# Four output projections of an attention block moved ahead of the scores on TensorE

## The chip, the cores and the metric

The kernel runs on one core of a Trainium2 chip. The metric is the device time of one execution in microseconds (us). A core has the engines PE (TensorE, matrix products), DVE (VectorE), ACT (ScalarE), POOL (GpSimd) and SP (SyncE, which issues the DMAs here). Each works through its own queue of instructions; semaphores order them against each other.

## The reference

Eight sequences of 128 tokens with 512 channels go through a gated cross-attention to a context and then through a gated feed-forward network (FFN) with 4-bit weights. Cut to what matters:

```python
# cross-attention, 32 query heads, 8 key/value heads, d = 128
q = rope(layernorm(x) @ Wq); k = rope(ctx @ Wk); v = ctx @ Wv
logits = 30 * tanh(q @ k.T * 0.0884 / 30)
weights = softmax(where(mask, logits, -1e30))
x = x + tanh(g_xattn) * ((weights @ v) @ Wo)
# FFN, weights (q - zero - 1) * scale, groups of 128 rows
h = layernorm(x)
x = x + tanh(g_ffn) * ((silu(h @ Wg) * (h @ Wu)) @ Wd)
```

## The kernel before, in words

Everything is float32 in accuracy: each operand of a matrix product is split into a rounded part (`_hi`) and the rest (`_lo`), and `split_matmul` (lines 50 to 54) makes one product of three matmuls. ACT makes the `_hi` part, DVE or POOL the `_lo` part.

The attention runs in 64 steps, one for each of 8 key/value heads g and 8 sequences b, step s = 8g + b (`SLOTS` = 64, `TAIL` = 56 is the first step of the last head). They are pipelined over slots, 0 to 66. Every engine has a function `slot(s)` that writes its instructions by hand in a fixed order, and `all_slots` calls it for each slot. On PE (line 1239) slot s does:

1. `transpose_k(s-1)`, one small matmul; the Q projection `make_q(s+4)`, 12 matmuls, if there is one left: `has_q_job(s)` is true up to slot 59; `make_kv(s)`, 12 shorter matmuls for keys and values of step s;
2. the scores of step s-1 into `ps_s`, 3 matmuls. They wait for the semaphore `qk_split`, raised by DVE's `kT_lo` (line 982) at the end of `split_qk`;
3. the P·V product of step s-2, after two matmuls into `ps_tot` for the row sums;
4. from slot 61 on, `norm2_T`, four transposes of the FFN's normalised input; in slots 65 and 66 the first gate and up matmuls of the FFN;
5. the output projection of step s-3 into `ps_o`, 12 matmuls. It waits for `a_split`, raised by POOL's `aT_lo` (line 548), and for `acc_done`.

The other engines in the last eight slots, in the order of their queues:

- ACT (line 704): `scale_share` (step s-4's projection out of `ps_o`), `round_q` and `round_k` of s-1, `round_p` of s-2, `aT_hi` of s-3, `v_hi` of s, `cap_and_exp` of s-1 (tanh and exponential), from slot 61 `norm2_hi`, and in slot 61 `round_ffn` (lines 653 and 654). `scale_share` waits for `o_done` and for the residual sum before.
- POOL (line 535): `add_share` (adds that share to the residual `acc`, line 533), `p_rest` (`p_lo` of s-2, line 526), `aT_lo` of s-3 (line 548), `apply_mask` of s-1 (line 472), `invert_std2` (line 497); in slot 60 also `scale` (line 503) and in slot 62 `rest` (lines 509 and 511), both for the FFN's first weights. `p_rest` waits for ACT's rounding of the masked probabilities of s-2.
- DVE (line 985): `split_qk` of s-1 (`qT_lo` line 980, `kT_lo` line 982), `norm2_apply` (`xn`, line 968), the rope of the keys, `moments2_of`, the reciprocal of the row sums and `attn` of s-2 (line 1028), transpose and row sums of the probabilities of s-1 (lines 1034 and 1037). In slots 59 and 61 it also unpacks FFN weights (lines 925 and 928) at the end.

The lines in which the waits of this text are written:

```python
# POOL, slot(s)
                    if TAIL <= s < SLOTS:
                        p_rest(s)
...
                        pool.wait_ge(a_rounded, s - 2)
                        nc.gpsimd.tensor_tensor(aT_lo[:], attn[:], aT_hi[:].bitcast(F32),
                                                ALU.subtract).then_inc(a_split, 1)
# ACT
                def round_p(s):
                    act.wait_ge(masked, s + 1)
# PE, scores in slot(s)
                        pe.wait_ge(qk_split, s)
```

Of the kernel before, what the change touches and what calls it, by code (L numbers as in the profile page):

```python
# [17 lines left out]
B = 8  # L18
T = 128
# [3 lines left out]
HG = 4  # L23
D = 128
GC = HG * D
SLOTS = KV * B
# [30 lines left out]
def flamingo_block(nc, x, ctx_in, mask, g_xattn, g_ffn, Wq, Wk, Wv, Wo,  # L57
# [16 lines left out]
    with ExitStack() as here:  # L74
# [225 lines left out]
        def runs(s):  # L300

            return 0 <= s < SLOTS
# [6 lines left out]
        with nc.Block() as block:  # L309
# [815 lines left out]
            def _(pe):  # L1125
# [110 lines left out]
                prep(7)  # L1236
                make_q(3)

                def slot(s):
                    if runs(s - 1) and s != SLOTS:  # L1240
                        transpose_k(s - 1)
                    if 0 < s and has_q_job(s):
                        make_q(s + AHEAD)
                    if runs(s):
                        make_kv(s)
                    if s == 0:
                        make_q(AHEAD)
                    if runs(s - 1):

                        pe.wait_ge(qk_split, s)  # L1250
                        wait(pe, tanh_done, s - 1)
                        split_matmul(nc, ps_s[:].rearrange("p (h t) -> p h t", h=HG), kT_hi[:], kT_lo[:],
                                     qT_hi[:], qT_lo[:], True, True).then_inc(s_done, 1)
                    if runs(s - 2):

                        vb = (s - 2) % 4
                        pe.wait_ge(p_split, s - 1)
                        wait(pe, norm_done, s - 2)
                        if s == 2:
                            pe.wait_ge(fold_done, 2)  # L1260
                        pe.wait_ge(p_summed, s - 1)
                        nc.tensor.matmul(ps_tot[:, 0:GC // 32], fold[:], partial[:], start=True, stop=True).then_inc(tot_done, 1)
                        mm = split_matmul(nc, ps_pv[:], v_hi[:, vb, :], v_lo[:, vb, :], p_hi[:], p_lo[:], True, True)
                        mm.then_inc(pv_done, 1)
                    if s == TAIL + 9:

                        pe.wait_ge(gate_centred, 1)
                        pe.wait_ge(w_split, 1)
                        pe.wait_ge(prep2_lo, HALF)
                        pe.wait_ge(q_roped, SLOTS)  # L1270
                        pe.wait_ge(qk_split, SLOTS)
                        gate_up(0, 0, 0, (0, 1))
                    if s == TAIL + 10:

                        gate_up(0, 0, 0, (2, 3))
                    if s >= TAIL + 5:
                        norm2_T(s - TAIL - 5)
                    if s == SLOTS - 1:
                        transpose_k(s)
                    if runs(s - 3):  # L1280

                        wp = ((s - 3) // B) % 2
                        if (s - 3) % B == 0:
                            pe.wait_ge(wo_split, ((s - 3) // B + 1) * HG)
                        pe.wait_ge(a_split, s - 2)
                        wait(pe, acc_done, s - 3)
                        for h in range(HG):
                            mm = split_matmul(nc, ps_o[:], aT_hi[:, h * T:(h + 1) * T],
                                              aT_lo[:, h * T:(h + 1) * T],
                                              wo_hi[wp][:, h, :], wo_lo[wp][:, h, :], h == 0, h == HG - 1)  # L1290
                        mm.then_inc(o_done, 1)
                    if s == TAIL + 10:
                        pe.wait_ge(norm_done, SLOTS)
                        norm2_T(6)
# [83 lines left out]
```

## Time and profile before

| | |
|---|---|
| median of 3 runs | 803.22 us |
| lowest and highest | 801.55 and 806.28 us |
| span of the profiled execution, first to last instruction | 802.9 us |
| mean granted TensorE clock | 0.980 |
| attention slots 60 to 63 in that execution | 561.1 to 605.6 us |

The span lies within the times of the runs, 0.3 us below their median. Times in the trace count from the first instruction. Matmuls are pipelined and a row's duration includes the time in the pipe, so the distance of two starts tells what one costs. The granted clock is a share of 2.4 GHz; 0.50 is the lower level, 1.2 GHz. A number behind an operation in brackets is the idle time of the engine ahead of it, with the instruction that ended it. "fp32r" is the rounded float format of the split parts.

### The profile page before, as it was taken

Reading aid. Unit: us, or ns where it says so; the run is one execution under the profiler, and the core shown is the slowest. Engines: PE = TensorE matmul, PEld = TensorE weight load, DVE = VectorE, ACT = ScalarE, POOL = GpSimd, SP = SyncE. Lnnn points to the kernel's source line nnn. Section 1 sums busy time; section 2 is a strip of 40 time slices with the busy share of each in tenths; the row PEclk is TensorE's granted clock in tenths of the full one; section 3 lists DMA queues with packets and bytes.
Section 4 is the critical chain, followed back from the end, with each engine's and each line's share of the span. In section 5 each row is a group of like instructions: output and inputs, shape, how many; then the busy total and the mean of one; then the engine's idle time right before and its main releaser. Section 6 shows DMA issues by size and latency. Waiting matters only on the chain.

```text
span 802.9 us, 11837 instructions
## 1 busy us (share of the span) xinstructions
PE 748.9 (93%) x3650; PEld 618.8 (77%) x3650; DVE 665.4 (83%) x1226; ACT 424.1 (53%) x823; POOL 478.6 (60%) x367
## 2 busy tenths in 40 slices
PE   3879999999999999999999999989668689999998
PEld 2657888888888888888888888878556468888786
DVE  7589999999999999999999999996887687787531
ACT  3475655665565556556556555545444344554520
POOL 4486666566566557556655755576766456656400
PEclk9999999999999999999999999999889899999999
DMA  8601002000200300020020003010110134442011
GB/s 287 199 0 54 1 27 106 0 27 2 105 2 27 105 0 27 5 102 21 8 104 2 27 29 104 8 41 0 26 38 1 46 87 97 102 105 48 0 66 39
DMA packets 57136, 41.70 MB, mean 52 GB/s; under 512 B 22938, under 2 KB 44442, under 8 KB 57082
## 3 DMA queue, kind: packets, MB, share of 16 engines
q1 hardware_dynamic: 57082, 41.03, 17.2%
q8 instruction: 27, 0.44, 0.2%
q14 instruction: 27, 0.22, 0.1%
HBM read 38.90 MB, written 2.11 MB: 51 GB/s over the span
## 4 chain that ended last, share of the span: by engine, by line
PE 85%; DVE 9%; issue 3%; POOL 2%; ACT 1%; DMA 0%; SPq 0%; DVEq 0%; ACTq 0%; POOLq 0%
PE ps_o L52 8%; PE ps_o L53 8%; PE ps_o L54 8%; PE bank_q L52 7%; PE bank_q L54 7%; PE bank_q L53 7%; PE ps_pv L52 3%; PE ps_s L52 3%; PE bank_kv L54 3%; PE bank_kv L52 3%; PE bank_kv L53 3%; PE ps_s L53 3%; PE ps_s L54 3%; PE bank_q L1147 3%; PE bank_q L1148 3%
## 5 line engine op out<-in xcount | busy, mean ns | idle before, releaser
L480 POOL TENSOR_TENSOR q_sin<-q_sin,q_tab 128x512 f32<-128x512 f32 x64 | 84.5, 1320 | 82.8 <-ACT q_sin L623 82.8
L472 POOL TENSOR_TENSOR probs<-probs,keepT 128x512 f32<-128x512 f32 x64 | 83.8, 1309 | 58.8 <-ACT probs L695 58.6
L548 POOL TENSOR_TENSOR aT_lo<-attn,aT_hi 128x512 fp32r<-128x512 f32 x64 | 85.7, 1338 | 51.8 <-ACT aT_hi L718 51.8
L52 PE MATMUL bank_q<-xT_hi,wq_hi 128*128 128x512 f32 x256 | 107.9, 421 | 3.0 <-DVE xT_lo L828 2.0
L52 PE MATMUL ps_o<-wo_hi,aT_hi 128*128 128x512 f32 x256 | 101.7, 397 | 1.8 <-POOL aT_lo L548 1.1
L980 DVE TENSOR_TENSOR qT_lo<-q_rot,qT_hi 128x512 fp32r<-128x512 f32 x64 | 97.0, 1515 | 6.9 <-ACT qT_hi L674 6.9
L53 PE MATMUL bank_q<-xT_lo,wq_hi 128*128 128x512 f32 x256 | 102.1, 399 | 0.0
L54 PE MATMUL bank_q<-xT_hi,wq_lo 128*128 128x512 f32 x256 | 102.0, 398 | 0.0
L53 PE MATMUL ps_o<-wo_lo,aT_hi 128*128 128x512 f32 x256 | 100.9, 394 | 0.0
L54 PE MATMUL ps_o<-wo_hi,aT_lo 128*128 128x512 f32 x256 | 100.7, 393 | 0.0
L622 ACT COPY q_sin<-bank_q 64x512 f32<-64x512 f32 x64 | 37.4, 584 | 49.3 <-PE bank_q L54 47.2
L52 PEld LDWEIGHTS bank_q<-xT_hi,wq_hi 128*128 128x128 f32 x256 | 49.1, 192 | 17.9 <-DVE xT_lo L828 2.4
L690 ACT ACTIVATE capped<-ps_s 128x512 f32<-128x512 f32 x64 | 38.3, 599 | 43.1 <-PE ps_s L54 43.0
L952 DVE SCALAR_TENSOR_TENSOR later_sum<-bank_q,gate_s,first_sum 128x512 f32<-128x512 f32 (+1 forms) x44 | 32.9, 748 | 33.5 <-PE bank_q L1148 20.1
L52 PEld LDWEIGHTS ps_o<-wo_hi,aT_hi 128*128 128x128 f32 x256 | 48.7, 190 | 13.1 <-POOL aT_lo L548 1.3
L54 PEld LDWEIGHTS bank_q<-xT_hi,wq_lo 128*128 128x128 f32 x256 | 48.7, 190 | 11.8
L54 PEld LDWEIGHTS ps_o<-wo_hi,aT_lo 128*128 128x128 f32 x256 | 48.8, 190 | 10.7
L53 PEld LDWEIGHTS ps_o<-wo_lo,aT_hi 128*128 128x128 f32 x256 | 48.8, 191 | 10.3
L53 PEld LDWEIGHTS bank_q<-xT_lo,wq_hi 128*128 128x128 f32 x256 | 49.1, 192 | 8.8
L520 POOL TENSOR_TENSOR gate_sum<-later_sum 128x512 f32<-128x512 f32 (+1 forms) x22 | 33.2, 1509 | 33.2 <-DVE later_sum L952 33.2
L841 DVE TENSOR_TENSOR bank_q<-bank_q,q_tab 128x512 f32<-128x512 f32 x64 | 44.1, 689 | 7.2 <-ACT q_sin L623 7.2
L1028 DVE TENSOR_TENSOR attn<-ps_pv,r_tot 128x512 f32<-128x512 f32 x64 | 44.3, 692 | 4.9 <-POOL aT_lo L548 2.2
(239 smaller groups left out, 2199.6 us busy)
## 6 DMA issues: line engine op xcount, KB each, us to landing
wo_raw<-in_Wo SPq DMA_DIRECT2D x8, 1024.0 KB, 5.4
wq_raw<-in_Wq SPq DMA_DIRECT2D x7, 1024.0 KB, 5.4
packed<-in_gate_q SPq DMA_DIRECT2D x40, 64.0 KB, 2.2
packed<-in_up_q SPq DMA_DIRECT2D x40, 64.0 KB, 2.2
packed<-in_down_q SPq DMA_DIRECT2D x10, 256.0 KB, 3.2
acc<-in_x SPq DMA_DIRECT2D x8, 256.0 KB, 5.1
wkv_raw<-in_Wk SPq DMA_DIRECT2D x8, 256.0 KB, 2.8
wkv_raw<-in_Wv SPq DMA_DIRECT2D x8, 256.0 KB, 3.2
```

The costliest lines, as they stand in the source:

```text
L52: nc.tensor.matmul(out, w_hi, m_hi, start=first, stop=False)
L53: nc.tensor.matmul(out, w_hi, m_lo, start=False, stop=False)
L54: return nc.tensor.matmul(out, w_lo, m_hi, start=False, stop=last)
L472: nc.gpsimd.tensor_tensor(pr, pr, keepT[:].unsqueeze(1).to_broadcast([P, HG, T]), ALU.mult).then_inc(masked, 1)
L480: nc.gpsimd.tensor_tensor(q_sin[:], q_sin[:], q_tab[:, 1, :].unsqueeze(1).to_broadcast([P, HALF, T]), ALU.mult).then_inc(q_sined, 1)
L520: nc.gpsimd.tensor_tensor(gate_sum[0:rows, half, :], later_sum[0:rows, 0, :], later_sum[0:rows, 1, :], ALU.add).then_inc(gate_summed, 1)
L548: nc.gpsimd.tensor_tensor(aT_lo[:], attn[:], aT_hi[:].bitcast(F32), ALU.subtract).then_inc(a_split, 1)
L622: nc.scalar.copy(q_sin[0:D // 2], q_banks[n % 2][D // 2:D])
L690: nc.scalar.activation(capped[:], ps_s[:], ACT.Tanh, scale=ATTN_MULT / MAX_ATTN).then_inc(tanh_done, 1)
L841: nc.vector.tensor_tensor(q_banks[n % 2], q_banks[n % 2], q_tab[:, 0, :].unsqueeze(1).to_broadcast([P, HALF, T]), ALU.mult).then_inc(q_cos ...
L980: nc.vector.tensor_tensor(qT_lo[:], q_rot[:, s % B // HALF, :, s % HALF, :], qT_hi[:].bitcast(F32), ALU.subtract)
L1028: nc.vector.tensor_tensor(attn[:], ps_pv[:], r_tot[:], ALU.mult).then_inc(norm_done, 1)
```

## The change

In slots 60 to 63 (`TAIL + 4 <= s < SLOTS`) PE runs the output projection of step s-3 between `make_kv(s)` and the scores of step s-1. In all other slots it stays where it was. Its waits go with it. No other engine's program is changed.

```diff
+                def project(s):
+                    wp = ((s - 3) // B) % 2
+                    if (s - 3) % B == 0:
+                        pe.wait_ge(wo_split, ((s - 3) // B + 1) * HG)
+                    pe.wait_ge(a_split, s - 2)
+                    wait(pe, acc_done, s - 3)
+                    for h in range(HG):
+                        mm = split_matmul(nc, ps_o[:], aT_hi[:, h * T:(h + 1) * T],
+                                          aT_lo[:, h * T:(h + 1) * T],
+                                          wo_hi[wp][:, h, :], wo_lo[wp][:, h, :], h == 0, h == HG - 1)
+                    mm.then_inc(o_done, 1)
+
                 def slot(s):
...
                     if s == 0:
                         make_q(AHEAD)
+                    if TAIL + 4 <= s < SLOTS:
+                        project(s)
                     if runs(s - 1):
...
                     if s == SLOTS - 1:
                         transpose_k(s)
-                    if runs(s - 3):
-
-                        wp = ((s - 3) // B) % 2
...
-                        mm.then_inc(o_done, 1)
+                    if runs(s - 3) and not TAIL + 4 <= s < SLOTS:
+                        project(s)
```

PE's queue in slot 61, from the last matmuls for keys and values (`bank_q`, step 61) on: the scores of step 60 are `ps_s`, the projection of step 58 is `ps_o`. Before:

```order
L52 MATMUL bank_q<-wkv_hi_83,cT_hi 128x256
L53 MATMUL bank_q<-wkv_lo_85,cT_hi 128x256
L54 MATMUL bank_q<-wkv_hi_83,cT_lo 128x256
L52 MATMUL ps_s<-qT_hi,kT_hi 128x512 [waits tanh_done,qk_split]
L53 MATMUL ps_s<-qT_lo,kT_hi 128x512
L54 MATMUL ps_s<-qT_hi,kT_lo 128x512
L1262 MATMUL ps_tot<-partial,fold 128x16 [waits p_summed,norm_done,p_split]
L52 MATMUL ps_pv<-p_hi,v_hi 128x512
L53 MATMUL ps_pv<-p_lo,v_hi 128x512
L54 MATMUL ps_pv<-p_hi,v_lo 128x512
L1169 MATMUL ps_x<-ident,xn 128x128 [waits xn2]
L1169 MATMUL ps_x<-ident,xn 128x128 x3
```

The same place with the change, the first matmuls of the projection:

```order
L52 MATMUL bank_q<-wkv_hi_83,cT_hi 128x256
L53 MATMUL bank_q<-wkv_lo_85,cT_hi 128x256
L54 MATMUL bank_q<-wkv_hi_83,cT_lo 128x256
L52 MATMUL ps_o<-wo_hi_86,aT_hi 128x512 [waits acc_done,a_split]
L53 MATMUL ps_o<-wo_lo_88,aT_hi 128x512
L54 MATMUL ps_o<-wo_hi_86,aT_lo 128x512
```

The `ps_o` block with its two waits now stands directly behind the keys and values. Its 12 matmuls end with the same `L54 MATMUL ps_o` form, and the scores follow:

```order
L54 MATMUL ps_o<-wo_hi_86,aT_lo 128x512
L52 MATMUL ps_s<-qT_hi,kT_hi 128x512 [waits tanh_done,qk_split]
L53 MATMUL ps_s<-qT_lo,kT_hi 128x512
L54 MATMUL ps_s<-qT_hi,kT_lo 128x512
L1276 MATMUL ps_tot<-partial,fold 128x16 [waits p_summed,norm_done,p_split]
```

Scores, row sums and P·V now stand behind the projection; in slot 60 and in slot 63 the move is the same. POOL's queue is the same before and after. From the mask of slot 61 to `aT_lo` of slot 62 it holds:

```order
L472 TENSOR_TENSOR probs<-probs,keepT 128x512 [waits exp_done]
L497 TENSOR_TENSOR rstd<-rstd,minus_half 128x1 [waits var2]
L533 TENSOR_TENSOR acc<-acc,share 128x512 [waits share_scaled]
L526 TENSOR_TENSOR p_lo<-probs,p_hi 128x512 [waits p_rounded]
L548 TENSOR_TENSOR aT_lo<-attn,aT_hi 128x512 [waits a_rounded]
```

The waits for `exp_done` and `p_rounded` stand ahead of `aT_lo`, which raises `a_split`; nothing moved here.

## Rows read from the trace of the kernel before

**Rows 1.** The page: busy time by engine, and the chain that ended last.

```profile
PE 748.9 (93%) x3650; PEld 618.8 (77%) x3650; DVE 665.4 (83%) x1226; ACT 424.1 (53%) x823; POOL 478.6 (60%) x367
...
PE 85%; DVE 9%; issue 3%; POOL 2%; ACT 1%; DMA 0%; SPq 0%; DVEq 0%; ACTq 0%; POOLq 0%
```

**Rows 2.** Timeline of PE: start, duration, operation, in brackets idle before and releaser.

```profile
558.35 0.40 PE L52 MATMUL ps_o<-wo_hi,aT_hi 128*128 128x512 f32 x1
...
560.86 0.39 PE L54 MATMUL ps_o<-wo_hi,aT_lo 128*128 128x512 f32 x1
...
568.01 0.79 PE L52 MATMUL ps_s<-qT_hi,kT_hi 128*128 128x512 f32 x1 [5.23 <-DVE kT_lo L982]
...
578.02 0.50 PE L52 MATMUL ps_s<-qT_hi,kT_hi 128*128 128x512 f32 x1 [1.36 <-DVE kT_lo L982]
...
590.16 0.79 PE L52 MATMUL ps_s<-qT_hi,kT_hi 128*128 128x512 f32 x1 [5.22 <-DVE kT_lo L982]
...
599.85 0.50 PE L52 MATMUL ps_s<-qT_hi,kT_hi 128*128 128x512 f32 x1 [1.35 <-DVE kT_lo L982]
...
605.59 0.39 PE L52 MATMUL ps_s<-qT_hi,kT_hi 128*128 128x512 f32 x1
...
613.43 0.29 PE L1262 MATMUL ps_tot<-partial,fold 128*128 128x16 f32 x2
```

**Rows 3.** Timeline of POOL in slots 60 to 63 and at the start of slot 64.

```profile
564.97 2.24 POOL L548 TENSOR_TENSOR aT_lo<-attn,aT_hi 128x512 fp32r<-128x512 f32 x1
571.03 1.28 POOL L472 TENSOR_TENSOR probs<-probs,keepT 128x512 f32<-128x512 f32 x1 [3.82 <-ACT probs L695]
...
572.81 2.14 POOL L503 TENSOR_TENSOR w_full<-w_full,scales 128x1024 f32<-128x1024 f32 x1
575.93 1.29 POOL L533 TENSOR_TENSOR acc<-acc,share 128x512 f32<-128x512 f32 x1 [0.98 <-ACT share L702]
...
578.87 1.47 POOL L548 TENSOR_TENSOR aT_lo<-attn,aT_hi 128x512 fp32r<-128x512 f32 x1
580.36 1.29 POOL L472 TENSOR_TENSOR probs<-probs,keepT 128x512 f32<-128x512 f32 x1
...
584.20 1.29 POOL L533 TENSOR_TENSOR acc<-acc,share 128x512 f32<-128x512 f32 x1 [2.03 <-ACT share L702]
...
587.12 2.24 POOL L548 TENSOR_TENSOR aT_lo<-attn,aT_hi 128x512 fp32r<-128x512 f32 x1
593.18 1.28 POOL L472 TENSOR_TENSOR probs<-probs,keepT 128x512 f32<-128x512 f32 x1 [3.82 <-ACT probs L695]
...
596.17 1.31 POOL L511 TENSOR_TENSOR wd_lo<-w_full,wd_hi 128x512 fp32r<-128x512 f32 x1
...
604.67 1.28 POOL L526 TENSOR_TENSOR p_lo<-probs,p_hi 128x512 fp32r<-128x512 f32 x1
```

**Rows 4.** Windows of slots 60 and 62: busy time by engine, then the granted clock (PEclk).

```profile
568.00:573.30 5.30, 5.29 (x14) 4.23 (x15) 4.41 (x13) 1.23 (x2) 2.27 (x3) 0.50 0.00 0
...
590.10:593.90 3.80, 3.74 (x11) 3.05 (x12) 3.66 (x13) 1.23 (x2) 0.71 (x1) 0.50 0.00 0
```

**Rows 5.** Timeline of ACT in slot 61 and at the start of slot 62.

```profile
581.71 0.62 ACT L654 CAST wd_hi<-w_full 128x512 fp32r<-128x512 f32 x1
583.43 0.69 ACT L702 ACTIVATE share<-ps_o,tgates 128x512 f32<-128x512 f32 x1 [1.11 <-PE ps_o L54]
```

**Rows 6.** Timeline of DVE: slot 60, and the work behind the last key split.

```profile
563.81 2.28 DVE L928 SCALAR_TENSOR_TENSOR w_full<-packed,zeros 128x1024 f32<-128x1024 uint32 x1
566.01 1.74 DVE L980 TENSOR_TENSOR qT_lo<-q_rot,qT_hi 128x512 fp32r<-128x512 f32 x1
...
604.21 0.28 DVE L982 TENSOR_TENSOR kT_lo<-bank_q,kT_hi 128x128 fp32r<-128x128 f32 x1
...
612.23 0.69 DVE L1037 TENSOR_REDUCE partial<-r_tot 128x16 f32<-128x512 f32 x1
```

**Rows 7.** Timeline of PE where the FFN's own work begins.

```profile
634.69 0.80 PE L1147 MATMUL bank_q<-xT_hi,gate_int 128*128 128x512 f32 x1 [1.40 <-DVE xT_lo L973]
```

More of the change, by code:

```diff
@@ L1279, in slot @@
                         transpose_k(s)
-                    if runs(s - 3):
-                        wp = ((s - 3) // B) % 2
[L1283 to L1290, printed above, removed]
-                        mm.then_inc(o_done, 1)
+                    if runs(s - 3) and not TAIL + 4 <= s < SLOTS:
+                        project(s)
                     if s == TAIL + 10:
```

## Prediction

> **What bounds the kernel now.** I read the page first: PE is busy 93% of the span, and the chain that ended last is 85% PE [rows 1]. So a microsecond in which PE does nothing costs nearly a microsecond. The last attention slots are the exception that the change aims at. In the timeline of PE, the scores of slots 60, 61, 62 and 63 start after idle times of 5.23, 1.36, 5.22 and 1.35 us, 13.2 us in all, each ended by DVE's key split at line 982 [rows 2]. In the earlier slots a Q projection of 12 matmuls fills that hole; from slot 60 on there is none. I name the work by its sequence number: slot s projects keys and values of s, makes the scores of s-1, the P·V product of s-2 and the output projection of s-3. As long as the projection comes last in the slot, nothing waits for it that is urgent.
>
> The question is then one of readiness. The moved projection waits for the semaphore a_split, which is raised by POOL's aT_lo at line 548. The POOL timeline [rows 3] tells when that comes. In slot 60 aT_lo runs from 564.97 to 567.21, while PE finished keys and values at 562.8 and the scores could go at 568.01 [rows 2]. So already in the first slot the moved work is ready only 0.8 us before the scores would be: 4.4 us of the hole can't be filled at all, and the 12 matmuls then stand in front of the scores.
>
> **The ring that the change closes.** In POOL's queue of one slot stand, in this order: add_share, p_lo, aT_lo, mask, rstd (the order excerpt shows it, and the change leaves it as it is). p_lo of slot s needs the probabilities of s-2, so the mask of s-2, so the exponentials, so the scores of s-2, which PE made in slot s-1. aT_lo stands behind p_lo in POOL's queue though it needs only older data. Before, the scores of s-1 waited for nothing of this. Now they stand on PE behind the projection, which waits for aT_lo, which waits behind p_lo, which waits for the scores of s-2. Each slot from 61 on is one turn of that ring, and its length is a sum of rows.
>
> **The terms.** The change adds and removes no instruction; four blocks of 12 matmuls move past 3+1+3 matmuls (and the four small transposes of norm2 in slots 61 to 63). No DMA and no instruction of ACT, DVE or POOL moves.
>
> - *Projection.* At the full clock 12 matmuls take 2.7 us: the first starts at 558.35, the last at 560.86, with a spacing of 0.23 [rows 2]. After the idle time of 5.2 us the granted clock was 0.50, the level of 1.2 GHz, for 5.3 us in slot 60 and 3.8 us in slot 62 [rows 4]; matmuls then cost about 0.43 us, so 12 take 5.1 us when all are slow, and 3.8 + (2.7 - 3.8×0.53) = 4.5 us when the slow stretch is 3.8 us. The holes before the moved projections are 4.5 us (slot 60: 562.8 to 567.3) and more (below), so I take 4.8, the middle, with 2.7 as the floor (the clock stays up) and 5.1 as the ceiling.
> - *Scores to mask.* 578.02 to 580.36, so 2.3 us at the full clock; 568.01 to 571.03, 3.0 us, at the half clock [rows 2, 3]. I take 2.3, since the projection ahead has by then used up most of the slow stretch; 3.0 is the ceiling.
> - *Mask to the end of the scaling of the FFN's first weights* (mask, rstd, scale, slot 60): 571.03 to 574.95, 3.9 us. *Mask to the end of wd_lo* (slot 62): 593.18 to 597.48, 4.3 us [rows 3].
> - *add_share, p_lo, aT_lo:* 575.93 to 580.34, 4.4 us in slot 61; 584.20 to 589.36, 5.2 us in slot 62 [rows 3]. These POOL operations are lengthened by DVE beside them: p_lo alone is 1.28 us [rows 3], so three alone would take about 3.8. I take the 4.4 as measured, since qT_lo and xn on DVE still have to run somewhere between mask and aT_lo.
>
> On that last choice a page can be weighed. In slot 60 aT_lo took 2.24 us, and DVE's w_full beside it 2.28 with qT_lo 1.74 right behind [rows 3, 6]. The Trainium skill (SBUF — State Buffer, SBUF: two separate sides) says that VectorE and GpSimd share a port pair which is an exclusive lock: the one that starts first holds it for its whole instruction and the other is blocked. By that rule DVE's short operations go in between POOL's wherever they fall, and the sum stays with 4.4; if they fell outside, two slots would each lose 0.6 us and the sum below would be 17.1 instead of 18.3.
>
> **The sum**, start to start, from the time of the unchanged start of slot 60:
>
> 1. Slot 60: aT_lo ends 567.2, projection 567.3 to 572.1. Scores at 572.1 instead of 568.0: 4.1 late.
> 2. Slot 61: mask 572.1+2.3 = 574.4, scale ends 578.3, aT_lo ends 582.7; projection 582.8 to 587.6. Scores at 587.6 instead of 578.0: 9.6 late.
> 3. Slot 62: here POOL's add_share waits for ACT, which still has the rounding of norm2 and of the first FFN weights before it: 578.02 to 582.33 is 4.3 us from the scores, and 0.8 us from the start of ACT's share (583.43) to POOL's add (584.20) [rows 2, 3, 5]. 587.6+4.3+0.8 = 592.7; plus 5.2 is 597.9; projection 598.0 to 602.8. Scores at 602.8 instead of 590.2: 12.6 late.
> 4. Slot 63: 602.8+2.3+4.3+4.4 = 613.8; projection 613.9 to 618.7. Scores at 618.7 instead of 599.9: 18.8 late.
> 5. Slot 64 gives a little back. The last scores no longer have a projection of 2.7 us ahead of them. The key split that they wait for ended at 604.49, 4.6 us behind the scores of slot 63, and the scores started at 605.59 [rows 2, 6]: 623.3 now, 17.7 late. DVE's own work behind the key split is 18.8 late without a break until the row sums of 612.92 [rows 6], which PE uses at 613.43 [rows 2], 0.5 us after they were done. So the tail is 18.8-0.5 = 18.3 us late.
>
> The holes ahead of the moved projections follow: from the scores of slot 61 to the hole of slot 62 PE had 584.94-578.02 = 6.9 us of work, 4.2 without the projection [rows 2]. So PE runs dry at about 576.3, 591.8 and 607.0, and waits 6.5, 6.2 and 6.9 us in slots 61, 62 and 63.
>
> From slot 65 on the order is the old one and everything shifts. PE starts the FFN after a wait for DVE's last xT_lo at 634.69 [rows 7], and that hangs on the same chain. The FFN's loads are not what it waits for there, so nothing gives the delay back. The sum is +18.3 us. The profiled execution has a span of 802.9 us, 0.3 below the median of the three runs, 803.22. Forecast: 803.2+18.3 = 821.5 us, 2.3% slower.
>
> **The rivals.**
>
> - *The clock stays up.* Same ring, but each projection costs 2.7 instead of 4.8: 4×2.1 = 8.4 less, +9.9, so 813.1 us. For it: the hole before the first moved projection is 4.5 us, shorter than the 5.2 after which the rows show the half clock. Against it: in slots 61 to 63 the holes are 6 to 7 us. The Trainium skill (Perfetto Trace Analysis, Matmul Optimizations) says that the engine scales with its use, so matmuls should run back to back in batches; by that rule moving a batch into a hole should keep the clock. Whether it does depends here on when the batch is ready, and the rows put that at the end of the hole. 10%.
> - *The lateness does not build up.* If some link of the ring had slack that I take for work, only slot 60's and part of slot 61's delay would remain, +4.1 to +9.6, so 807 to 813. Against it: each link is a wait in the code and the sum has no idle POOL in slot 61 or 63. 5%.
> - *The holes are filled: faster.* The place is slots 60 to 63, PE. If a_split were up when keys and values are done, the projections would fit into the holes: 2.7+2.7 in the long ones and 1.36+1.35 in the short ones, 8.2 us saved, 795.0 us. It decides at 562.8 in slot 60: aT_lo would have to end by then, and it ended at 567.21 [rows 3]. In slots 61 to 63 it would have to come before p_lo in POOL's queue, which the build doesn't do. 3%.
> - *The change does nothing*, because PE lets ready scores pass the waiting projection: 803. In the hole before 568.01 nothing of the later matmuls ran, though the projection behind them was free for its last 0.8 us [rows 2, 3]; I take PE's queue to be in order. The page on TensorE in the Trainium skill (TensorE: Matmul & The Clock Gate, Step-by-step: what each phase is for) says the same: only weight loads are pulled ahead. 3%.
>
> **How the numbers follow.** The main case has 79%. A measurement of this kernel can tell 0.5%, about 4 us, from no change: its three runs lie between 801.55 and 806.28. Main case, warm clock and slow build-up are slower by more than that, except for the lower end of the build-up case: 92% slower. 5% within 0.5% (no effect, and that lower end), 3% faster. The range: from below the warm clock (813.1) with DVE's operations out of the way (1.2 less), 812; to all-slow projections (4×0.3) and half-clock scores in two slots (2×0.7) with a microsecond for contention, +18.3+3.6, 825. What lies outside are the last three rivals.
>
> **What the profile after would show.** Right: on PE, in slots 61, 62 and 63, idle times of 6 to 7 us ahead of the first ps_o matmul, released by POOL's aT_lo at line 548, and none of size ahead of the scores; the scores of these slots near 587.6, 602.8 and 618.7; a granted clock near 0.5 in most of each projection; ACT, DVE and POOL idle while it runs; PE starting the FFN near 653. Wrong: matmuls of 0.23 us spacing in the moved blocks (warm clock), or aT_lo ahead of p_lo, or a shift at the FFN's start that later shrinks. If the scores of slot 61 are less than 9 us late, the ring or one of its terms is mis-sized.

## The result, and the profile after

| | before | changed |
|---|---|---|
| median of 4 runs | 804.31 us | 825.47 us |
| lowest and highest | 801.55 and 806.28 us | 825.25 and 826.85 us |
| ratio, 95% interval | | 1.0262 [1.0239, 1.0285] |
| span of the profiled execution | 802.9 us | 823.5 us |
| mean granted clock | 0.980 | 0.967 |

The change makes the kernel 2.6% slower, 19 to 23 us. Forecast were 821.5 us and a range up to 825. The sign and the mechanism of the first slots were right, the time lies 0.5 us above the range.

The page of the changed kernel, busy time by engine and the chain that ended last:

```profile
PE 755.1 (92%) x3650; PEld 624.4 (76%) x3650; DVE 666.1 (81%) x1226; ACT 423.9 (51%) x823; POOL 478.7 (58%) x367
...
PE 85%; DVE 6%; POOL 5%; issue 2%; ACT 2%; DMA 0%; SPq 0%; DVEq 0%; ACTq 0%; POOLq 0%
```

PE's share falls by a point and the chain's share on POOL rises from 2% to 5% [rows 1]. PE's busy time even grows from 748.9 to 755.1 us with the same 3650 instructions: some of them ran at the lower clock. The waits between 561 and 640 us name the new stall (total us, how often, the longest):

```profile
POOL probs L472 <- ACT probs L695: 28.6, 4, 8.0
...
PE ps_o L52 <- POOL aT_lo L548: 24.8, 4, 7.2
```

PE's projection (`ps_o`) waited 24.8 us for POOL's `aT_lo` in four pieces, and POOL's mask 28.6 us for the exponentials. Before, the four long holes of PE were 13.2 us in all and stood ahead of the scores [rows 2]. The timeline of PE shows where the new ones are; the number in brackets is the idle time ahead of the row:

```profile
568.17 0.80 PE L52 MATMUL ps_o<-wo_hi,aT_hi 128*128 128x512 f32 x1 [4.47 <-POOL aT_lo L548]
...
573.46 0.63 PE L52 MATMUL ps_s<-qT_hi,kT_hi 128*128 128x512 f32 x1
...
584.33 0.79 PE L52 MATMUL ps_o<-wo_hi,aT_hi 128*128 128x512 f32 x1 [7.18 <-POOL aT_lo L548]
...
588.85 0.39 PE L52 MATMUL ps_s<-qT_hi,kT_hi 128*128 128x512 f32 x1
...
598.67 0.80 PE L52 MATMUL ps_o<-wo_hi,aT_hi 128*128 128x512 f32 x1 [6.07 <-POOL aT_lo L548]
```

```profile
602.86 0.39 PE L52 MATMUL ps_s<-qT_hi,kT_hi 128*128 128x512 f32 x1
...
613.71 0.80 PE L52 MATMUL ps_o<-wo_hi,aT_hi 128*128 128x512 f32 x1 [7.11 <-POOL aT_lo L548]
...
618.85 0.39 PE L52 MATMUL ps_s<-qT_hi,kT_hi 128*128 128x512 f32 x1
...
623.17 0.50 PE L52 MATMUL ps_s<-qT_hi,kT_hi 128*128 128x512 f32 x1 [2.01 <-DVE kT_lo L982]
...
626.43 0.58 PE L1276 MATMUL ps_tot<-partial,fold 128*128 128x16 f32 x2 [2.31 <-DVE partial L1037]
...
628.99 0.78 PE L52 MATMUL ps_o<-wo_hi,aT_hi 128*128 128x512 f32 x1
...
633.37 0.29 PE L1276 MATMUL ps_tot<-partial,fold 128*128 128x16 f32 x2
```

```profile
654.62 0.79 PE L1147 MATMUL bank_q<-xT_hi,gate_int 128*128 128x512 f32 x1 [1.40 <-DVE xT_lo L973]
```

In each of the four slots the projection begins after a hole of 4.5 to 7.2 us, released by `aT_lo`, and the scores follow 4.2 to 5.3 us later with no wait of their own. POOL's queue from the mask of slot 60 to `aT_lo` of slot 61 shows what fills such a hole:

```profile
576.08 1.29 POOL L472 TENSOR_TENSOR probs<-probs,keepT 128x512 f32<-128x512 f32 x1 [7.95 <-ACT probs L695]
577.32 0.56 POOL L497 TENSOR_TENSOR rstd<-rstd,minus_half 128x1 f32<-128x1 f32 x1
577.85 2.13 POOL L503 TENSOR_TENSOR w_full<-w_full,scales 128x1024 f32<-128x1024 f32 x1
579.93 1.71 POOL L533 TENSOR_TENSOR acc<-acc,share 128x512 f32<-128x512 f32 x1
581.61 1.45 POOL L526 TENSOR_TENSOR p_lo<-probs,p_hi 128x512 fp32r<-128x512 f32 x1
583.02 1.26 POOL L548 TENSOR_TENSOR aT_lo<-attn,aT_hi 128x512 fp32r<-128x512 f32 x1
```

From 576.08 to 584.28 POOL is busy without a gap: mask, rstd, FFN scaling, add_share, p_lo, aT_lo. PE's block starts at 584.33. The windows over the four moved blocks and over the projection of slot 64 (busy time by engine, then the granted clock, the third number from the end):

```profile
568.10:573.40 5.30, 5.22 (x12) 4.13 (x13) 2.65 (x10) 0.00 (x0) 0.02 (x1) 0.50 0.00 0
584.30:588.80 4.50, 4.47 (x12) 3.56 (x13) 0.00 (x0) 0.00 (x0) 0.00 (x0) 0.60 0.41 115
598.60:602.80 4.20, 4.13 (x12) 3.36 (x13) 3.70 (x12) 0.00 (x0) 0.01 (x1) 0.64 0.00 0
613.70:618.80 5.10, 5.09 (x12) 4.03 (x13) 0.00 (x0) 0.00 (x0) 0.00 (x0) 0.51 0.00 0
628.90:633.30 4.40, 4.40 (x15) 3.55 (x14) 4.05 (x8) 0.88 (x2) 1.79 (x2) 0.61 0.02 4
```

The granted clock is 0.50 to 0.64 there, mostly the lower level of 1.2 GHz.

To compare traces below I count from the start of slot 60 in each, taken at ACT's first `share` of that slot (561.28 us before, 562.20 changed). The lateness of a slot is that of ACT's tanh, which starts when the scores are done. For the changed kernel against the first profile of before: 4.1, 9.8, 11.0, 18.0 us in slots 60 to 63, 16.8 in slot 64, and 19.0 at the start of the FFN (654.62 against 634.69 [rows 7], less 0.9 us that slot 60 itself starts later).

### The profile page after: what moved, and what is told of

Same layout as the page of the kernel before. It is cut to its first block, busy times and chain, and to the rows that moved or that the text cites. A ratio compares the mean times of both kernels' runs of the same rounds, so it can differ in the third digit from the quotient of the medians.

```text
span 823.5 us, 11837 instructions
## 1 busy us (share of the span) xinstructions
PE 755.1 (92%) x3650; PEld 624.4 (76%) x3650; DVE 666.1 (81%) x1226; ACT 423.9 (51%) x823; POOL 478.7 (58%) x367
## 3 DMA queue, kind: packets, MB, share of 16 engines
q1 hardware_dynamic: 57082, 41.03, 16.8%
## 4 chain that ended last, share of the span: by engine, by line
PE 85%; DVE 6%; POOL 5%; issue 2%; ACT 2%; DMA 0%; SPq 0%; DVEq 0%; ACTq 0%; POOLq 0%
PE ps_o L52 8%; PE ps_o L53 8%; PE ps_o L54 8%; PE bank_q L52 7%; PE bank_q L53 7%; PE bank_q L54 7%; PE ps_pv L52 3%; PE ps_s L52 3%; PE ps_s L53 3%; PE bank_kv L54 3%; PE bank_kv L52 3%; PE bank_kv L53 3%; PE ps_s L54 3%; PE bank_q L1147 3%; PE bank_q L1148 2%; PE ps_pv L53 2%
## 5 line engine op out<-in xcount | busy, mean ns | idle before, releaser
L52 PE MATMUL ps_o<-wo_hi,aT_hi 128*128 128x512 f32 x256 | 105.6, 412 | 25.5 <-POOL aT_lo L548 24.8
L53 PE MATMUL ps_o<-wo_lo,aT_hi 128*128 128x512 f32 x256 | 104.1, 406 | 0.0
L54 PE MATMUL ps_o<-wo_hi,aT_lo 128*128 128x512 f32 x256 | 103.5, 404 | 0.0
L54 PE MATMUL bank_q<-xT_hi,wq_lo 128*128 128x512 f32 x256 | 102.0, 398 | 0.0
L52 PEld LDWEIGHTS ps_o<-wo_hi,aT_hi 128*128 128x128 f32 x256 | 50.7, 198 | 37.9 <-POOL aT_lo L548 25.6
L54 PEld LDWEIGHTS ps_o<-wo_hi,aT_lo 128*128 128x128 f32 x256 | 50.7, 198 | 11.4
L53 PEld LDWEIGHTS ps_o<-wo_lo,aT_hi 128*128 128x128 f32 x256 | 50.9, 199 | 10.7
L54 PEld LDWEIGHTS bank_q<-xT_hi,wq_lo 128*128 128x128 f32 x256 | 48.7, 190 | 11.8
```

The costliest lines, as they stand in the source:

```text
L52: nc.tensor.matmul(out, w_hi, m_hi, start=first, stop=False)
L53: nc.tensor.matmul(out, w_hi, m_lo, start=False, stop=False)
L54: return nc.tensor.matmul(out, w_lo, m_hi, start=False, stop=last)
```

## The experiments

Times are ratios to runs of the kernel before on the same chip, and the same in us at 804. "At the FFN" is the lateness of the FFN's start against the first profile of before, counted from slot 60. That profile holds a collision of DVE and POOL which a second profile of the same program lacks (see "The kernel before, twice"): against the second, every kernel is later by 0.6, 3.4, 2.6 and 2.6 us in slots 61 to 64 and by 2.7 us at the FFN. Three other kernels, "slot 60 only", "slot 62 only" and "slot 63 only", lack it too.

| kernel | ratio [95%] | us | at the FFN |
|---|---|---|---|
| changed | 1.0262 [1.0239, 1.0285] | +21.1 | +19.0 |
| moved in slot 60 only | 1.0024 [1.0003, 1.0045] | +1.9 | +0.8 |
| slot 61 only | 1.0120 [1.0076, 1.0164] | +9.7 | +7.1 |
| slot 62 only | 1.0111 [1.0078, 1.0144] | +8.9 | +7.3 |
| slot 63 only | 1.0082 [1.0058, 1.0106] | +6.6 | +4.5 |
| slots 60 and 61 | 1.0167 [1.0143, 1.0192] | +13.4 | +11.4 |
| slots 60 and 62 | 1.0139 [1.0095, 1.0184] | +11.2 | +10.2 |
| changed, POOL's aT_lo first | 1.0171 [1.0125, 1.0216] | +13.7 | +11.7 |
| changed, ACT's aT_hi first | 1.0255 [1.0213, 1.0297] | +20.5 | +19.0 |
| changed, both first | 1.0156 [1.0110, 1.0201] | +12.5 | +10.9 |
| before, both first, nothing moved | 1.0091 [1.0058, 1.0125] | +7.3 | +6.6 |
| slots 60 and 62, both first | 1.0092 [1.0072, 1.0113] | +7.4 | +4.9 |
| the same with fillers | 1.0082 [1.0061, 1.0104] | +6.6 | +3.7 |
| changed, fillers in the holes | 1.0144 [1.0099, 1.0190] | +11.6 | +11.4 |
| changed, fillers in slot 64 | 1.0239 [1.0196, 1.0282] | +19.2 | +18.4 |
| before, fillers in two holes | 0.9998 [0.9984, 1.0011] | -0.2 | -2.4 |
| before, a second time | 0.9982 [0.9957, 1.0007] | -1.4 | -2.7 |

### Which slots pay

The edit is the condition of the move, in both places where it stands:

```diff
-                    if TAIL + 4 <= s < SLOTS:
+                    if s == TAIL + 4:
                         project(s)
```

Slot 60 alone.

> Only slot 60 keeps the moved projection; slots 61 to 63 have the old order. Theory (the delay is passed on only through a ring: scores, mask, p_lo, aT_lo, projection, next scores): without a moved projection in slot 61 the ring is cut; the scores of slot 60 come some 5 us late (start near 573.4 instead of 568.0, as in the changed kernel), but PE then has the projection behind it, so most of that comes back in the next slot. Total +0.5 to +3 us over the kernel before. Rival (each moved block costs its own share, a quarter of the whole): +5 us (a quarter of 21).

Measured: 1.0024. The scores of slot 60 were 3.6 us late, those of the next slots 2.0, 0.0, 0.8 and 0.8. By that the lateness fades, as the theory has it. Against the second profile of before it does not: 3.6, 2.6, 3.5, 3.4 and 3.4. This kernel's own slot 61 has no collision, so the second is the like one to compare with. In time slot 60 costs +1.9 us, between 0.2 and 3.6, which does not tell the two apart. Slots 60 and 61:

> The changed kernel with the projection moved in slots 60 and 61 only. Theory (one turn of the ring): the scores of slot 61 are 9.9 us late as in the changed kernel, the ring is cut behind it, and DVE's queue hands most of it on: +6 to +10 us. Beside slot 60 alone (+2) this is far more than twice as much. Rival (each moved block costs the same): twice slot 60 alone, +4.

Measured (with `TAIL + 4 <= s < TAIL + 6`): +13.4 us, above the expected 6 to 10; the lateness stays at 9.4, 7.9, 8.7 and 9.8 us behind the moved blocks and is not given back. The next kernel was to decide between ring and number of blocks: as many moved blocks, no two of them neighbours.

```diff
-                    if TAIL + 4 <= s < SLOTS:
+                    if s in (TAIL + 4, TAIL + 6):
                         project(s)
```

> The changed kernel with the projection moved in slots 60 and 62 only, POOL's and ACT's orders untouched: as many moved blocks as in slots 60 and 61, but no two in neighbouring slots. Ring theory: the ring is cut in slots 61 and 63, each delay of the scores of about 4 us fades behind its slot as it did for slot 60 alone: +1 to +4 us over the kernel before. Rival (what counts is the number of moved blocks): as slots 60 and 61, +11 to +13 us.

Measured: +11.2 us, the rival's value, so the ring theory missed. Slot 60's 3.6 us fall to 2.0 as before, but slots 62 to 64 show 6.5, 3.7 and 8.7. PE of that kernel:

```profile
594.27 0.80 PE L52 MATMUL ps_o<-wo_hi,aT_hi 128*128 128x512 f32 x1 [3.69 <-POOL aT_lo L548]
...
598.46 0.39 PE L52 MATMUL ps_s<-qT_hi,kT_hi 128*128 128x512 f32 x1
...
608.11 0.61 PE L1276 MATMUL ps_tot<-partial,fold 128*128 128x16 f32 x2 [2.61 <-POOL p_lo L526]
```

The projection of slot 62 starts behind a hole of 3.69 us and its scores come 6.5 us late. One slot on, PE stands 2.61 us in front of the row sums and P x V, released by POOL's p_lo at line 526. The trace suggests a path that I had left out: late scores make a late mask, POOL then works off its queue up to p_lo, and P x V of the next slot waits for it, whether or not a projection is moved there. In slot 64 the scores of this kernel are 8.7 us late. So I formed the other theory, that each moved block pays by itself, and ran the other slots alone, with `s == TAIL + 5`, `TAIL + 6` and `TAIL + 7` as the condition.

> The changed kernel with the projection moved in slot 61 only. Scores of slot 60 on time, projection of slot 61 behind a hole of 3.7 us, then 2.7 to 4.8 us: scores of slot 61 are 5 to 7 us late. Theory A (ring: a delay grows only where moved blocks stand in neighbouring slots, alone it fades): +0 to +3 us over the kernel before. Theory B (a late block of scores is paid for through mask, POOL's queue and P x V, whatever is moved behind it; only slot 60 has room, because DVE's unpacking hides it): +5 to +9 us.

Measured: +9.7 us, just above the range of theory B and far from that of A. The PE rows:

```profile
580.14 0.79 PE L52 MATMUL ps_o<-wo_hi,aT_hi 128*128 128x512 f32 x1 [3.68 <-POOL aT_lo L548]
...
585.43 0.63 PE L52 MATMUL ps_s<-qT_hi,kT_hi 128*128 128x512 f32 x1
...
596.32 0.80 PE L52 MATMUL ps_s<-qT_hi,kT_hi 128*128 128x512 f32 x1 [6.83 <-DVE kT_lo L982]
```

The block starts behind a hole of 3.68 us (before, 1.36 stood ahead of the scores [rows 2]), takes 5.3 us, and the scores are 7.1 us late, then 5.7, 5.5, 5.5 in the slots behind, which all have the old order.

> Moved in slot 62 only. From slots 60 and 62 together (10.2 us at the start of the FFN) less slot 60 alone (0.8): theory B gives +7 to +10 us. Theory A (two blocks two slots apart still coupled, alone it fades): +1 to +4.

Measured: +8.9 us, theory B.

> Moved in slot 63 only. Behind it comes slot 64, which then has no projection ahead of the last scores. Theory B: scores of slot 63 late by 5 to 7 us, 1 us of it won back in slot 64: +4 to +8 us. If B holds for all slots and nothing is coupled, the four single prices add up to 19 us at the start of the FFN, the changed kernel's; if they add up to clearly more or less, the slots are coupled.

Measured: +6.6 us, theory B. The four single prices add up to 27.1 us in time (19.7 at the FFN against the first profile of before, 30.3 against the second, which is 2.7 us earlier; see below), the changed kernel costs 21.1 (19.0; 21.7). By the times, and more so by the second profile, the blocks cost less together than one by one; by the first they simply add. The interval of the 27.1 is some 5 us, so that the slots save something together is likely and not shown. The pairs show nothing of it: slots 60 and 61 cost 13.4 us where the singles give 11.6, slots 60 and 62 11.2 where they give 10.8. What the times do show is that the four together cost no more than their sum: neighbours do not add a price of their own, as a ring that alone passes the delay on would have it.

### The link

POOL's order, in slots 60 to 63, the projection moved as in the change:

```diff
+                    if TAIL + 4 <= s < SLOTS:
+                        a_rest(s)
                     if TAIL <= s < SLOTS:
                         p_rest(s)
...
-                    if runs(s - 3):
+                    if runs(s - 3) and not TAIL + 4 <= s < SLOTS:
+                        a_rest(s)
```

`a_rest` is the wait and the instruction of `aT_lo`.

> The changed kernel, with POOL's aT_lo ahead of p_lo in slots 60 to 63; ACT's order stays. Theory: aT_lo no longer waits for p_lo (1.3 to 1.7 us in each slot), but the mask of the slot before, add_share and ACT's round_p still stand ahead, so the ring stays and each turn gets 1.3 to 1.7 us shorter; in slot 60 the projection starts 2.5 to 3 us sooner. +10 to +15 us over the kernel before. Rival (the move itself costs, whatever the ring's length): as the changed kernel, +21.

Measured: +13.7 us, 7.4 less than the changed kernel, as the theory has it. PE's holes ahead of the blocks were 2.29, 5.93, 3.91 and 5.88 us instead of 4.47, 7.18, 6.07 and 7.11, 6.8 us less in all. The clock had no part in it: the four blocks took 4.4, 4.8, 5.3 and 4.7 us, 19.2 in all against 19.1 in the changed kernel. Then ACT alone, `aT_hi` ahead of `round_p`:

```diff
+                    if TAIL + 4 <= s < SLOTS:
+                        round_a(s)
                     if runs(s - 2) and s != SLOTS + 1:
                         round_p(s - 2)
```

> The changed kernel with only ACT's aT_hi ahead of round_p in slots 60 to 63, POOL's order untouched. Theory (the link is POOL's queue, where aT_lo stands behind p_lo): no gain, and p_lo starts up to 0.5 us later; +19 to +22 us over the kernel before, as the changed kernel. Rival (ACT's queue is the link): +10 to +14, as with both reorderings.

Measured: +20.5 us, no gain. Both together:

> As the one before, and on ACT the rounding aT_hi ahead of round_p in slots 60 to 63. Theory: the ring still goes through mask and add_share on POOL (acc_done is the projection's other wait), so little is won over the version with POOL alone: +9 to +14 us over the kernel before, and projections in slots 61 to 63 still start behind holes of 4 us or more. Rival (p_lo behind round_p is the whole ring, so both reorderings cut it): holes gone, at most +3, or faster than before.

Measured: +12.5 us, with holes of 2.28, 5.94, 3.87 and 5.88 us. What is left in the hole of slot 61 is POOL's queue again, busy without a gap from the mask (572.10 us) to the end of `aT_lo` (579.08). So one link is POOL's p_lo; the others, mask, FFN scaling and add_share ahead in the same queue, are read from the trace, no run took them out. What does the reordering cost without any moved block (both diffs above, on the kernel before)?

> The kernel before with both reorderings of slots 60 to 63 (aT_lo ahead of p_lo, aT_hi ahead of round_p) and no projection moved. It prices the reordering in the runs with it: p_lo is 1.3 to 1.7 us later, which P x V waits for in slots 61 and 63 only: +1 to +4 us. Rival (p_lo has room everywhere): 0.

Measured: +7.3 us, far above the expected 1 to 4. The lateness is 0 in slot 60, below 0 in slots 61 and 62 (-0.6 and -1.1; 0.0 and 2.3 against the second profile), then 1.1, 4.9 in slot 64 and 6.6 at the FFN. p_lo 1.3 to 1.7 us later is paid for more than once. A version that cuts the ring, with the reordering in the slots of the two long holes only, was my candidate for a faster kernel. In all three places, PE, POOL and ACT:

```diff
-                    if TAIL + 4 <= s < SLOTS:
+                    if s in (TAIL + 4, TAIL + 6):
```

> The projection is moved ahead of the scores in slots 60 and 62 only, the two with the long holes (DVE unpacks FFN weights there), and only there aT_lo goes ahead of p_lo on POOL and aT_hi ahead of round_p on ACT. Slots 61 and 63 have the old order, so that the ring is cut. Theory: the projection is ready 2.3 us into the hole (measured with the reordering in all four slots) and ends at about the time of DVE's key split, the scores are at most 1 us late, and the slots behind start with up to 2.7 us less work on PE: -5 to -1 us against the kernel before. Rival (moving a projection ahead of the scores costs in itself): +5 us or more.

Measured: +7.4 us, wrong. Its scores were 0.9 us early in slot 61 and 2.4 late in slot 62; in slot 63 PE waited 2.37 us for p_lo, and slot 64 was 3.6 us late. With fillers (described under the clock, below), 9 in each of the two slots:

```diff
+                    for i in range({4: 9, 6: 9}.get(s - TAIL, 0)):
```

> As the one before, with 9 matmuls that nobody reads in the first 2 us of each of the two holes, so that the granted clock stays up. Theory: the blocks behind the holes run at the full clock: -7 to -2 us against the kernel before, 1 to 4 us below the one without fillers. Rival (the time there hangs on DVE alone): the same as the one without fillers.

Measured: 1.0082 against 1.0092, no difference that the intervals bear out. No version that I tried beats the kernel before.

### The clock

Matmuls that nobody reads are put into the holes ahead of the moved blocks, into the bank `bank_q`, which is free there:

```diff
+                    for i in range({4: 17, 5: 29, 6: 24, 7: 28}.get(s - TAIL, 0)):
+                        if i == 0:
+                            pe.wait_ge(q_roped, SLOTS)
+                        nc.tensor.matmul(bank_q[:], cT_hi[:, B - 1, 0, :], cT_hi[:, B - 1, :, :], start=True, stop=True)
                     if TAIL + 4 <= s < SLOTS:
                         project(s)
```

> The changed kernel with matmuls that nobody reads, into a bank that is free there, in the holes ahead of the four moved projections (17, 29, 24 and 28 of them). Only the granted clock should change. Theory (of the 19 us lost in slots 60 to 66, about half is the ring's own length and about half the half clock in the moved blocks and in the projection of slot 64): the blocks take 2.7 us instead of 4.2 to 5.3, so +10 to +13 us over the kernel before. Rival A (the clock is a side effect, the ring alone sets the time): +20 or more. Rival B (the clock is nearly everything): +5 or less.

Measured: +11.6 us. The window over the moved block of slot 61 in this kernel, the other three read the same:

```profile
581.30:584.10 2.80, 2.73 (x12) 2.28 (x13) 0.00 (x0) 0.00 (x0) 0.01 (x1) 1.00 0.42 101
```

12 matmuls in 2.73 us at a granted clock of 1.00, against 4.2 to 5.3 us in the changed kernel. The fillers end 0.65 to 0.85 us before the blocks, which still wait for `aT_lo`, so they are not in the way. The four blocks are 7.7 us shorter in all, and at the start of the FFN 7.6 of 19.0 us are gone. The other 11.4 remain with the clock up: the wait for `aT_lo` and the block itself, ahead of the scores. The same in the holes of slot 64 alone, 7 matmuls ahead of the last scores and 9 ahead of the row sums:

```diff
+                    if s == SLOTS:
+                        for i in range(7):
+                            nc.tensor.matmul(bank_q[:], cT_hi[:, B - 1, 0, :], cT_hi[:, B - 1, :, :], start=True, stop=True)
                     if runs(s - 1):
...
+                    if s == SLOTS:
+                        for i in range(9):
+                            nc.tensor.matmul(bank_q[:], cT_hi[:, B - 1, 0, :], cT_hi[:, B - 1, :, :], start=True, stop=True)
                     if runs(s - 2):
```

> The changed kernel with 7 and 9 matmuls that nobody reads in the two holes of slot 64 (2.0 us ahead of the last scores, 2.3 us ahead of the row sums). Theory (the 2.2 us that the tail still loses behind the last scores come from the half clock in the projection of slot 64, 4.4 us instead of 2.9): that block takes 2.9 us again, and the FFN starts 1 to 2 us sooner than in the changed kernel: +17.5 to +19.5 us over the kernel before in time, +17.0 to +18.0 at the start of the FFN. Rival (the loss behind the scores is DVE's or POOL's queue): +19 at the start of the FFN, as in the changed kernel.

Measured: +18.4 us at the FFN, between the two. The block and what follows it:

```profile
628.84 0.50 PE L52 MATMUL ps_o<-wo_hi,aT_hi 128*128 128x512 f32 x1
...
632.60 0.36 PE L1282 MATMUL ps_tot<-partial,fold 128*128 128x16 f32 x2 [0.74 <-DVE partial L1037]
```

The block now takes the 2.9 us that it took before, but PE then waits 0.74 us for DVE's row sums. From the last scores to the FFN the lateness grows by 1.4 us instead of 2.2. So 0.8 us are the clock's. The rest stands in DVE's queue. Its work from `qT_lo` to the row sums has no gap in the kernel before, in the changed one and in this one, but one operation in it got longer. Before, changed, and with fillers in slot 64:

```profile
607.58 0.54 DVE L968 TENSOR_SCALAR xn<-acc,moments,rstd 128x512 f32<-128x512 f32 x1
```

```profile
626.21 1.10 DVE L968 TENSOR_SCALAR xn<-acc,moments,rstd 128x512 f32<-128x512 f32 x1
...
631.42 0.69 DVE L1037 TENSOR_REDUCE partial<-r_tot 128x16 f32<-128x512 f32 x1
```

```profile
626.50 1.15 DVE L968 TENSOR_SCALAR xn<-acc,moments,rstd 128x512 f32<-128x512 f32 x1
...
631.76 0.69 DVE L1037 TENSOR_REDUCE partial<-r_tot 128x16 f32<-128x512 f32 x1
```

DVE's key split is 17.7 us late in the changed kernel and its row sums 18.3, 0.6 more by `xn`. POOL's mask ran beside `xn` there (625.77 to 627.03); that it made it longer no run tests.

And in the kernel before, 19 fillers each in the holes of slots 60 and 62:

```diff
+                    for i in range({4: 19, 6: 19}.get(s - TAIL, 0)):
```

> The kernel before, order untouched, with 19 matmuls that nobody reads in the holes of slots 60 and 62. Only the clock changes. Theory: 5.3 and 3.8 us of the half clock go, of which half is lost time: -5 to -2 us. Rival (DVE sets the time in those slots, PE's speed does not matter): within 1 us of the kernel before.

Measured: 0.9998 [0.9984, 1.0011]: the rival. PE's clock doesn't matter there. The -2.4 us at the FFN are +0.3 against the second profile of before.

### The kernel before, twice

```diff
 AHEAD = HALF
+AGAIN = True
```

> The kernel before once more, for a second profile. In its first profile the stretch from the FFN's start to the end took 168.2 us, in that of every other kernel 168.7 to 169.3. If that is chance (the phase in which the half clock falls there), the second profile lies at 168.7 or above, or the half clock there differs between profiles; if it is a price of the change, the second shows 168.2 again. The start of slot 60 lies between 561 and 563.5 us if its place is chance, too.

The constant is used nowhere. Measured: the stretch behind the FFN's start took 168.7 us, 0.5 more than in the first profile, and slot 60 started at 562.1, 1.0 later. Both are chance: the stretch behind the FFN's start is 168.6 to 169.3 us in every other profile, and slot 60, ahead of which all kernels are the same, starts up to 2.2 us later than in the first. The second profile showed something else that I had not asked for. DVE in slots 61 and 62 of the first profile:

```profile
584.28 1.76 DVE L925 SCALAR_TENSOR_TENSOR gate_int<-packed,zeros 128x512 fp32r<-128x512 uint32 x1
585.97 2.28 DVE L928 SCALAR_TENSOR_TENSOR w_full<-packed,zeros 128x1024 f32<-128x1024 uint32 x1
588.17 1.74 DVE L980 TENSOR_TENSOR qT_lo<-q_rot,qT_hi 128x512 fp32r<-128x512 f32 x1
```

and of the second:

```profile
584.68 0.68 DVE L926 SCALAR_TENSOR_TENSOR gate_int<-packed,zeros 128x512 fp32r<-128x512 uint32 x1
585.28 1.22 DVE L929 SCALAR_TENSOR_TENSOR w_full<-packed,zeros 128x1024 f32<-128x1024 uint32 x1
586.62 1.57 DVE L981 TENSOR_TENSOR qT_lo<-q_rot,qT_hi 128x512 fp32r<-128x512 f32 x1
```

with POOL's add_share of slot 62:

```profile
586.16 1.48 POOL L534 TENSOR_TENSOR acc<-acc,share 128x512 f32<-128x512 f32 x1 [3.61 <-ACT share L703]
```

The two unpacking instructions and the query split took 1.76, 2.28 and 1.74 us in the one and 0.68, 1.22 and 1.57 in the other. In the first profile POOL's add_share started at 584.20 [rows 3], 0.1 us ahead of the unpacking, and p_lo and aT_lo behind it ran beside DVE; in the second it started 1.5 us behind the start of the unpacking, when that was nearly through. PE's projection of slot 61 came later, too, first profile and second:

```profile
580.39 0.50 PE L52 MATMUL ps_o<-wo_hi,aT_hi 128*128 128x512 f32 x1
```

```profile
581.49 0.78 PE L53 MATMUL ps_o<-wo_hi,aT_hi 128*128 128x512 f32 x1
...
588.44 0.50 PE L53 MATMUL ps_s<-qT_hi,kT_hi 128*128 128x512 f32 x1 [1.55 <-DVE kT_lo L983]
```

The projection of slot 61 began at the full clock in the first (0.50 us for its first matmul), and at the half clock in the second (0.78). Counted from slot 60, it ended 1.0 us later, and ACT's share and POOL's add_share, which wait for it, 0.9 us later; DVE began 0.6 us sooner. So the two unpackings and POOL missed each other almost wholly, and the scores of slot 62 were 3.4 us earlier: the hole ahead of them is 1.55 us instead of 5.22. The FFN started 2.7 us earlier. Two more kernels have the old order up to this place, slot 62 only and slot 63 only. The latter shows:

```profile
584.55 0.68 DVE L925 SCALAR_TENSOR_TENSOR gate_int<-packed,zeros 128x512 fp32r<-128x512 uint32 x1
585.15 1.22 DVE L928 SCALAR_TENSOR_TENSOR w_full<-packed,zeros 128x1024 f32<-128x1024 uint32 x1
```

Both lack the collision (0.68 and 1.22 us), and in both the projection of slot 61 began at the half clock, as in the second profile. So the collision is in one of four such executions, the one with the full clock there. The three without it ran on one chip; the chip of the first isn't on record, so a difference between chips isn't ruled out. That the clock tipped it is read from these traces; no run tested it by itself, and the kernel with fillers in slots 60 and 62 lacks the collision with the clock at 1.00. The Trainium skill (SBUF — State Buffer, SBUF: two separate sides) describes the port pair of VectorE and GpSimd as an exclusive lock held for a whole instruction; the durations agree with that, 2.28 us beside POOL against 1.22 alone. So does the order in the first profile: POOL's add_share, begun 0.1 us sooner, ended at 585.49, and DVE's first unpacking, 0.68 us alone, 0.55 us behind that.

## Why the prediction was off

**What bounds the kernel, and readiness: right.** The moved block of slot 60 waited for `aT_lo` behind a hole of 4.47 us; 4.5 was forecast. The holes of slots 61 to 63 are 7.18, 6.07 and 7.11 us; 6.5, 6.2 and 6.9 were forecast.

**The sum's five steps: right within 1.1 us.** The forecast counts the start of the scores. For slots 60 to 64 it has 4.1, 9.6, 12.6, 18.8 and 17.7 us of lateness; measured at the same place are 4.5, 9.9, 11.8, 18.1 and 16.7 (at ACT's tanh, as in the tables above, 4.1, 9.8, 11.0, 18.0 and 16.8). The projection's 4.8 us were 5.3, 4.5, 4.2 and 5.1. The 4.4 us for add_share, p_lo and aT_lo were 4.35 us in slot 61 (579.93 to 584.28). On the page that was weighed there: p_lo and aT_lo were shorter than before (1.45 and 1.26), but add_share longer (1.71 instead of 1.29), so DVE's operations did fall between POOL's, and the sum stayed. There is luck in slot 62: its row of before holds the collision, and so does the changed kernel; against the second profile the same slot is 14.4 us late, not 11.0.

**The step that failed is the end of the sum: step 5, the tail, and the base that the sum was put on.** Neither is large, and with either as measured the time would have lain within the range.

*The base, 1.5 us.* The text says that the profiled execution has a span "0.3 us below the median of the three runs" and adds 18.3 to 803.2. In every run listed with both, the time is 1.8 us above the span (825.31 for 823.5). So that execution stood for some 804.7, an estimate, as none of the listed times is its own, and 1.5 above the median of three. A fourth run alone took the median to 804.31. The forecast also took slot 62's hole of 5.22 us as a property of the kernel; one execution in four had it. Against the second profile the changed kernel is 21.7 us late at the FFN, against the first 19.0, and the times say 21.1. Which of the two is the usual one isn't shown: the first, by its span, lies near the medians of before (804.3, and 805.1 in the last series), the second's 803.7 below them.

*The tail, 0.7 us, and its path.* The text has DVE's work behind the key split 18.8 us late up to the row sums, with 0.5 us to spare before PE uses them, so 18.3. Measured, the key split was 17.7 late and the row sums 18.3; but PE used them at 633.37, 19.0 us late, 1.3 us after they were done. The text says "From slot 65 on the order is the old one and everything shifts"; but slot 64, which lost its projection ahead of the scores, got two holes of 2.01 and 2.31 us, PE's clock fell, and its remaining projection took 4.4 us instead of 2.9. So PE's half clock, a term that was put at nothing in slot 64, set when the row sums were used, and not DVE; from the last scores to the FFN the lateness grew by 2.2 us (16.8 to 19.0 at the tanh) where the forecast had 0.6. The fillers show 0.8 us of that as the clock's; with them PE waits for DVE again, as forecast.

**The 0.9 us ahead of slot 60 and the 0.7 behind the FFN's start** belong to no step: the kernel before shows 1.0 and 0.5 of them in its second profile.

Added up, the changed kernel's span is 802.9 + 0.9 + 19.0 + 0.7 = 823.5, and its time 825.3. The forecast had 802.9 + 18.3 and 0.3. Of the 4.0 us between them 1.5 are the distance from span to time, 0.7 the end of the tail (19.0 for 18.3), and 1.6 the chance of the two profiles (0.2 is left from one run to the median).

**The ring.** As a description of the changed kernel's waits it holds: each hole is ended by `aT_lo`, and taking p_lo out from ahead of it gave back 7.4 us. As the cause of the total it was said too strongly. A moved block costs 7 to 10 us in slots 61 to 63 even alone, with the old order in the slot behind it, and the four together cost no more than their sum. That what follows late scores (mask, POOL's queue, P x V, DVE's unpacking) passes the lateness on is read from the waits. Slot 60 costs least, 1.9 us; why, stays open.

**The rivals.** *The clock stays up* was priced at +9.9 us; the fillers, which make it so, give +11.4 at the FFN. In the changed kernel it did not stay up. *The lateness does not build up*: false, it grows from 4.5 to 18.1 us over the four slots, and little of it is given back. *The holes are filled* and *the change does nothing*: false, each block starts when a hole of 4.5 to 7.2 us ends, and PE did not run the scores ahead of it.

## What to carry to other kernels

Before a block is moved into an idle hole, look up when its operands are ready, and what stands ahead of their producer in the producer's queue; a hole that the block can't enter until it ends makes everything behind the block late by the block's full length, here at the half clock. Take a second profile of the kernel before when the argument rests on one slot: here one execution held a collision of two engines that another lacked, worth 2.7 us. Set the sum on the median only after looking at how the span of that execution stands to its own time.

## What the runs showed of the hardware

Of two executions of the kernel before, the one in which a projection ran at the half clock was the faster: POOL came later, kept out of DVE's way, and the next scores came 3.4 us sooner. That the clock was the cause isn't shown. DVE's unpacking of 128x1024 took 1.22 us alone and 2.28 beside POOL, its unpacking of 128x512 0.68 and 1.76. In slot 64 of the changed kernel the granted clock was 1.00 between the holes of 2.01 and 2.31 us (623.1 to 624.1) and 0.50 right behind the second (626.4 to 628.9), and the projection there took 4.4 us instead of 2.9. In the second profile of before it fell to 0.50 within slot 61 (580.4 to 583.0), while PE was busy and its last hole was one of 1.35 us, ended at 578.42; in the first it stayed at 1.00 behind the like hole. Fillers in the holes kept it at 1.00 and gave 7.6 us back where the blocks stood ahead of the scores, and nothing where DVE's work set the time.
